# Two-stage attention on one core: last turns of the probabilities behind the next channel scores, VectorE's copies behind their maxima, and the stacked values sent batch by batch ahead of the loads of the next pair but one

## The reference

```python
enc = ctx[:, :124, :];  ca = ctx[:, 124:, :]
hs = mha(x @ Wq, enc @ Wk, enc @ Wv)                    # 8 heads of 40
ca_q1 = einsum('btc,th->bch', ca, Wq_ca)[:, picked, :]  # 128 of 192 channels
ca_hs1 = mha(ca_q1, x, x)                               # "channel" attention
ca_hs2 = mha(ca_hs1 @ Wq, ca @ Wk_ca, ca @ Wv_ca)       # 4 keys only
out = (hs + ca_hs2) @ Wout + b_out + x
```

## Time and profile before

| | before |
|---|---|
| median of three runs | 269.14 us |
| the profiled execution, own time | 267.8 us |
| its span in the trace | 265.7 us |
| PE busy | 231.2 us (87%) |
| DVE busy | 200.1 us (75%) |
| ACT busy | 113.5 us (43%) |
| POOL busy | 52.9 us (20%) |
| PE in the chain that ended last | 59% |
| DVE in that chain | 23% |
| DMA and SP's issuing in that chain | 4% and 4% |
| mean granted clock of TensorE | 0.968 of full |

### The profile page before, as it was taken

The page is one execution under the profiler, slowest core; times in us unless marked ns, Lnnn a source line. Parts: engine busy times, 40 slices in busy tenths (PEclk is TensorE's granted clock), DMA queues, the critical chain, the costliest instruction groups (busy, mean ns, idle before and its releaser), DMA issues.

```text
span 265.7 us, 5654 instructions
## 1 busy us (share of the span) xinstructions
PE 231.2 (87%) x1756; PEld 214.4 (81%) x1770; DVE 200.1 (75%) x547; ACT 113.5 (43%) x406; POOL 52.9 (20%) x135
## 2 busy tenths in 40 slices
PE   0289879999759997999799979997999799989984
PEld 0279767889648996899789978997899789987983
DVE  2764958779825897769897889788878887887683
ACT  3234634152405173337434733463445345424451
POOL 3230080033200332012500350035003500300000
PEclk9999977999968997999999999999999999999999
DMA  7992022027921410052005100520043002000101
GB/s 226 259 271 102 12 63 83 2 56 162 195 41 48 154 56 0 27 173 62 0 25 172 56 0 11 182 60 0 0 142 110 0 0 99 0 0 2 49 0 49
DMA packets 12180, 19.59 MB, mean 74 GB/s; under 512 B 1462, under 2 KB 8470, under 8 KB 12166
## 3 DMA queue, kind: packets, MB, share of 16 engines
q1 hardware_dynamic: 11343, 18.30, 24.8%
q10 hardware_dynamic: 823, 1.11, 1.5%
HBM read 14.17 MB, written 2.62 MB: 63 GB/s over the span
## 4 chain that ended last, share of the span: by engine, by line
PE 59%; DVE 23%; issue 6%; DMA 4%; SPq 4%; ACT 1%; DVEq 1%; ACTq 0%; POOL 0%
PE scores L1197 11%; PE bank_d L1222 10%; PE bank_d L1278 7%; PE bank_d L1049 6%; PE bank_a L1049 5%; DVE k_blocks L773 5%; SPq L396 4%; DVE neg_max L793 3%; PE turned L1044 3%; PE bank_d L1093 2%; DMA wca_t<-in_Wq_ca 2%; PE turned L1185 2%; DVE ca_less L681 2%; PE bank_d L1225 2%; DMA vw_stack<-vw_part 2%
## 5 line engine op out<-in xcount | busy, mean ns | idle before, releaser
L611 ACT ACTIVATE probs<-scores,neg_max 128x124 f32<-128x124 f32 x128 | 44.6, 377 | 12.3 <-DVE neg_max L793 12.3
L793 DVE TENSOR_REDUCE neg_max<-scores 128x4 f32<-128x512 f32 (+1 forms) x64 | 41.3, 676 | 4.0 <-PE scores L1169 1.9
L1049 PE MATMUL bank_a<-xT_r,wq_r 128*120 128x256 f32 (+1 forms) x192 | 29.1, 305 | 11.4 <-DVE xT_r L708 11.4
L600 ACT ACTIVATE probsT<-turned 128x512 f32<-128x512 f32 x32 | 17.4, 594 | 42.4 <-PE turned L1185 24.2
L1049 PEld LDWEIGHTS bank_a<-xT_r,wq_r 128*120 128x120 f32 (+1 forms) x192 | 25.8, 196 | 11.5 <-issue 11.4
L1222 PEld LDWEIGHTS bank_d<-xg,probsT 128*128 128x128 f32 x256 | 30.3, 193 | 2.8 <-issue 2.7
L1222 PE MATMUL bank_d<-xg,probsT 128*128 128x33 f32 x256 | 30.1, 272 | 2.5 <-ACT probsT L600 2.5
L1225 PE MATMUL bank_d<-v_sb,probsT 124*128 124x40 f32 x256 | 31.3, 278 | 0.0
L1225 PEld LDWEIGHTS bank_d<-v_sb,probsT 124*128 124x128 f32 x256 | 30.7, 192 | 0.0
L611 ACT ACTIVATION_READ_ACCUMULATOR probs<-scores,neg_max 128x1 f32 x128 | 28.1, 220 | 0.0
L1197 PE MATMUL scores<-k_blocks,qT 120*128 120x372 f32 (+2 forms) x96 | 24.6, 394 | 0.5 <-issue 0.2
(11 more groups left out here) (128 smaller groups left out, 401.8 us busy)
## 6 DMA issues: line engine op xcount, KB each, us to landing
xT<-in_x_cols SPq DMA_DIRECT2D x8, 384.0 KB, 3.8
x_h<-in_x_heads SPq DMA_DIRECT2D x8, 360.0 KB, 3.6
x_sb<-in_x SPq DMA_DIRECT2D x8, 320.0 KB, 3.3
vw_stack<-vw_part SPq DMA_DIRECT2D x16, 160.0 KB, 4.5
out<-out_sb SPq DMA_DIRECT2D x16, 160.0 KB, 1.8
ctxT<-in_ctx_cols SPq DMA_DIRECT2D x8, 256.0 KB, 4.0
wqT<-in_WqT ACTq DMA_DIRECT2D x1, 506.2 KB, 7.4
wq<-in_Wq ACTq DMA_DIRECT2D x1, 480.0 KB, 4.6
```

Of the source, the lines that this page charges most:

```text
L600: nc.scalar.activation(probsT[:, 4 * half:4 * half + 4, :], turned[half].rearrange("k (h q) -> k h q", h=4), ACT.Exp) \
L611: last = nc.scalar.activation(probs[:, h, 0:keys], scores[half][:, k * keys:(k + 1) * keys], ACT.Exp, bias=neg_max[:, h:h + 1], accum_out= ...
L793: v.tensor_reduce(neg_max[:, 4 * half:4 * half + 4], scores[half][:, 0:4 * keys].rearrange("q (h k) -> q h k", h=4), AX.X, ALU.max, negate ...
L1049: ins = mm(dst, stationary(w, half, c), moving(w, half, c), start=first and i == 0, stop=last and i == len(steps) - 1)
```

## The change

The change has three parts. On PE, `channel_scores` of the next pair stands ahead of `turn_probs` of unit 3, with a wait of its own for both halves of unit 3's exponentials. On DVE, `maxima` of the next unit 0 stands ahead of `turned_copy` of unit 3. On SP, the 16 DMAs of the stacked values go batch number by batch number with two semaphores, so that pair 1 waits for the first eight alone, and they stand ahead of the first pair's `body`, that is ahead of the loads of pair 2, instead of behind it.

```diff
-            body(At(0, 0, 0, "first"))
-
             sp.wait_ge(d_drained, RING_D.no(At(0, 0, 0, "first"), "VW3")[0] + 1)
-            for slot, part in enumerate(VW_PART):
-                for r in range(4):
+
+            for r in range(4):
+                for slot, part in enumerate(VW_PART):
                     sp.dma_start(
                         vw_stack[HT * slot:HT * slot + HT].bitcast(F32)
                             .rearrange("p (n s) h -> p n s h", s=4)[:, :, r, :],
-                        vw_parts[part][HT * r:HT * r + HT].bitcast(F32)).then_inc(vw_stacked, 16)
+                        vw_parts[part][HT * r:HT * r + HT].bitcast(F32)).then_inc(vw_stacked[r // 2], 16)
+
+            body(At(0, 0, 0, "first"))
...
                 norm(at, 2)
+                if more:
+                    maxima(unit(at, 4), S)
                 turned_copy(unit(at, 3), KEYS)
                 if more:
-                    maxima(unit(at, 4), S)
                     split_max(at.next(), 0)
...
-                pe.wait_ge(vw_stacked, 16 * 16)
+                pe.wait_ge(vw_stacked[0], 16 * 8)
+                if at == "epilogue" or at.b > 1:
+                    pe.wait_ge(vw_stacked[1], 16 * 8)
...
                 weigh(at, 2)
+                if more:
+                    got_d(at, "MsT")
+
+                    pe.wait_ge(exped, unit(at, 3) * 2 + 2)
+                    channel_scores(unit(at, 4), at.next(), 0)
                 turn_probs(unit(at, 3), KEYS)
                 if more:
-                    got_d(at, "MsT")
-                    channel_scores(unit(at, 4), at.next(), 0)
```

More of the change, by code:

```diff
@@ L284, in attention @@
         vw_high = sem("vw_high")
-        vw_stacked = sem("vw_stacked")
+        vw_stacked = [sem("vw_stacked0"), sem("vw_stacked1")]
         def g_out(masked, src, r):
```

## The result

The changed kernel took 274.63, 275.45, 281.80 and 281.86 us, median 278.62 us; the kernel before, with one run more, 268.49 us. The runs of the changed kernel lie in two groups, and the comparison takes the lower one: ratio 1.0261, 95% interval 1.019 to 1.033. The change makes the kernel slower; whether by more than two per cent the interval leaves just open. The profiled execution is the fastest, 274.63 us, 6.8 us above the one of before.

The account below looks back on a forecast made before the run. No single engine bounds it: the chain runs 59% through PE and 23% through DVE. 267.8 us (profiled before) + 5.4 lost in pair 1 - 0.8 gained in seams = 272.4, plus half of 1.3: 273.0 us, range 269.5 to 276.5.

Parts of the forecast that it names:

- The wait that goes: Pair 1: PE's wait on the stacked values disappears; token scores at 74.6 us if nothing else waited, gaining 6.4 us.
- The wait that comes: Pair 1: pair 2's xT load, queued behind 16 DMAs, lands at 77.2 us; ACT waits, weighing starts at 79.9.
- The clock in pair 1: PE's clock low for 5.0 us after the weighing starts; token scores 6.5 us later (bounds 4.37, 7.7), 5.4 us lost.
- The seams' own length: Six middle-pair seams: the pause before DVE's split goes, 0.13 us each (bounds 0 and 0.14), 0.8 us gained.
- The clock in the seams: Seams between pairs: the sum had no term for clock falls there, only the 0.8 us gain.
- C: Rival, faster: ACT isn't held at pair 1's head, the whole 6.4 us counts; 260.6 or 261.2 us, chance 0.03.
- B: Rival, pair 1: xT lands at 79.05, clock low until the token scores; 275.5 or 276.1 us, chance 0.17.
- D: Rival, seams: later copies hold up unit 3's weighing, 0.5 us in each of six seams; 276.8 us, chance 0.02.

Follow-up runs that it names:

- e4_batchwise: Kernel before with the stacked values sent batch by batch with two semaphores, behind pair 2's loads, seams as before; 262.86 us, ratio 0.984.
- e2_sp_only: Kernel before with the SP part alone, plus PE's two waits for it; 274.55 us, ratio 1.0283.
- e10: Changed kernel with pair 2's loads ahead of the stacked values, plus 7 unread transposes at the end of each pair but the last; 257.36 us, ratio 0.963.
- e11: Kernel before with stacked values batch by batch behind the loads, plus 7 unread transposes at the end of each pair but the last; 260.56 us, ratio 0.973.
- e14_after_warm: Changed kernel plus 7 unread transposes at the end of each pair but the last; 270.60 us, ratio 1.012.
- e1_seams_only: Kernel before with the moves on PE and DVE alone, SP as before; median 275.82 us, ratio 1.023.
- e3_loads_first: Changed kernel with SP's body of the first pair put back ahead of the stacked values; median 263.38 us, ratio 0.981.
- e8: Kernel before with one more wait on POOL: its low parts of ctx start after DVE's split of the maxima; median 272.11 us.
- e5: Kernel before with the PE move alone (channel scores ahead of the last turns); 294.16 us.
- e6: Kernel before with the DVE move alone (maxima ahead of the copies); 291.91 us.
- e7: Kernel before with the SP part alone, plus 76 unread transposes at the end of PE's first pair; 273.95 us, ratio 1.017.

## Why the prediction was right, and where it was wrong

The direction and the main mechanism were right: slower, because pair 2's loads are queued behind the stacked values and ACT waits for them at the head of pair 1. The size was too small. The forecast of 273.0 us is 3.9 us above the 269.14 of before, and by the ratio the loss is about 7; the likeliest class, within two per cent (0.63), is only just inside the interval. The profiled execution (274.6) lies inside the range, the median (278.6) 2.1 us above its upper end. That the former is so near is in part luck, as two errors in pair 1 have opposite signs. Step by step:

- **The wait that goes.** Right. e4_batchwise shows it alone: no wait in front of the projection, and token scores of pair 1 at 75.21 us, where the step had 74.6.
- **The wait that comes.** Right in kind. `high_x` started at 76.13 us, where I had the landing at 77.2; that is 4.1 us after the issue and not 5.4, so the landing was put 1.1 us too late. The queue behind the stacked values cost only about 1 us over the 3.0 of an idle queue. From there to the weighing it was 2.56 us against my 2.7.
- **The clock in pair 1.** The size was off, and this made up for the step above. I had 5.0 us of low clock behind the start of the weighing and 6.5 us to the token scores. It was low for 8.6, and the token scores came 87.34 - 78.69 = 8.65 us later, more even than my bound of 7.7. The return of the clock 5.0 us after PE resumed, which I took over from before, is no constant. And the factor 1.76 from a pair of weight loads is too small for the weighing, whose 16 small matmuls took 3.62 us instead of 1.87, 1.94 times as long. The loss was 6.35 us at this milestone instead of 5.4. In e2_sp_only, which has this part alone, it was 86.63 - 80.99 = 5.64 us there and 7.3 us in all, so some of its loss arises later; the runs do not show where for certain.
- **The seams' own length.** Mis-sized: 0.7 us a seam instead of 0.13. The prediction had named a move of more than 0.3 us a seam as a sign that it is wrong, and on this step it was. The pause in front of the split was read rightly (it went, 0.23 us with the overlap of the neighbours). Missing was the 0.52 us of the split's last operation. Its row, with 0.72 us for eight elements, was in the trace, and I did not ask which operation of POOL it ran beside. As e10 against e11 shows, the moves are worth 3.2 us, not 0.8.
- **The clock in the seams.** The term that the sum put at nothing, and the one that puts the median above the range. I took the seam's shortening as a gain at a constant clock, though the trace of before had one seam with a fall, holding its slow weight loads. The moves brought more falls: two more in the profiled execution, and enough in others for 282 us. The difference between the changed kernel and e14_after_warm is this term: 8.0 us by the medians, 3.7 by the ratios. What the moves cost net is not one number. Against e2_sp_only it is (278.6 - 268.5) - 7.3 = 2.8 us by the medians and nothing by the ratios (1.026 and 1.028). Without the SP part it is 8.5 us (e1_seams_only), with the loads ahead 0.5 (e3_loads_first against e4_batchwise). The 0.8 us of gain that the sum had for them came only where the pauses were filled, and there it was 3.2.
- **The rivals.** C is excluded: ACT was held, and e3 and e4 show that the removed wait pays only with the loads ahead. B came nearest. Its low clock to the token scores was there, though with an early landing. D gave a loss in the seams, by another mechanism than the one that it named: the later copies hold up nothing (the third weighing starts as soon as the value projections are through).

What stays open is why the clock falls in one seam and not in the next. Three kernels with a shorter seam (e1, e8, the changed one) and two with a longer one (e5, e6) all had more falls than the kernel before. The pause of 0.81 us in front of the product is there in all of them, with a fall and without. In the profiled executions, filling it removes all falls of the seams in three kernels and four of six in the fourth, and in e11_batchwise_warm the pauses of 0.49 us stay without harm. This shows that the falls need PE's idle time in the seam; which property of a seam decides is not.

## What to carry to other kernels

When a transfer is put ahead of others in one queue, look up every consumer of those others: a load that was harmless at 38 us was the head of another engine's list at 61. Before a wait is filled or shortened by tenths of a microsecond on a busy TensorE, look at the granted clock in that place. If it falls there in even one period of the trace, the clock can be worth more than the tenths, as here, and a few dummy transposes into a free bank are the cheapest test and here also the cure. An operation on VectorE that takes three times what its size asks for is worth a look at what GpSimd does in that moment.

## What the runs showed of the hardware

- In a kernel whose PE is otherwise busy, the granted clock went from 2.4 to 1.2 GHz in or right behind some of the seams in which PE stood for 0.81 us in front of one product (one seam before, three after the change), and in e5_pe_swap in each seam from that to pair 2 on, where it stood 1.17 and 0.81 us within two microseconds (23.7 us slower than before by the medians). Once low, it stayed so for 3 to 10 us, in e1_seams_only for 10 us with PE busy all the time.
- 16 matmuls of 33 columns with a weight load of 128 each took 1.87 us at the full clock and 3.62 at the lower.
- An operation of VectorE with both inputs in SBUF, 0.19 us long, took 0.72 us when it began just behind a GpSimd operation, and ended with it.
- A load of 384 KB from HBM, issued right behind 16 copies of 160 KB within SBUF that kept the DMA engines full, was there 4.1 to 4.7 us after its issue (the changed kernel, e2, e7), against 3.0 with idle engines.
